# Products of gathered points with their weights: weights copied to PSUM, one instruction for three

## The chip, the cores and the metric

The kernel runs on one core of a Trainium2 chip. Its time is the device time of one launch in microseconds, the median of the runs shown. The profile is of one execution with the hardware profiler on. Engines: TensorE (PE in the profile; PEld its weight loads), VectorE (DVE), ScalarE (ACT), GpSimd (POOL), SyncE (SP).

## The reference

Eight images of 56 x 56 pixels and 128 channels go through four layers. Layers 0, 2 and 3 are deformable convolution blocks; for each pixel, 4 groups x 9 points are read from the projected image at computed places, each as 4 neighbours with bilinear weights, and summed under a softmax mask:

```python
x0 = jnp.floor(ix); y0 = jnp.floor(iy); wx1 = ix - x0; wy1 = iy - y0
samp = corner(y0, x0, (1-wy1)*(1-wx1)) + corner(y0, x0+1, (1-wy1)*wx1) + corner(y0+1, x0, wy1*(1-wx1)) + corner(y0+1, x0+1, wy1*wx1)
y = jnp.einsum('nghwpc,nhwgp->nhwgc', samp, mask).reshape(N, H, W, C) @ w_out + b_out
x = x + gamma1 * layer_norm(y, ...)
x = x + gamma2 * layer_norm(gelu(x @ w_fc1 + b_fc1) @ w_fc2 + b_fc2, ...)
```

Layer 1 is a state space block: four directions, 256 channels, 16 states, with a linear recurrence along all 3136 pixels:

```python
h = h * exp(dt_t[..., None] * A) + (dt_t * u_t)[..., None] * B_t[:, :, None, :]
y = einsum('bkdn,bkn->bkd', h, C_t)
```

All is computed in 32-bit floats.

## The kernel before

**Two streams of work.** There are 24 gather stages (three layers by eight images), and per image one scan of layer 1. The scan of an image is cut into 28 pieces (4 directions x 7 chunks of 448 pixels) by 16 states: 448 scan steps an image, 3584 in all. Gather stages and scan steps of different images run beside each other. The order is written out beforehand: a planner (class `Planner`) emits one list of items, and each engine's program goes through the same list and emits its own part of each item, so the order on each engine is fixed. Semaphores connect the engines.

**A gather stage.** 25 tiles of pixels (24 of 128, one of 64), each in thirds of 12 parts, so 74 units a stage and 1776 in all. POOL (`gpsimd_program`, line 730) issues for each part an indirect DMA that fetches, by an index per partition taken from the SBUF tile d_idx, 128 rows of 512 bytes (4 neighbours x 32 channels) from a table in HBM into the slot d_g; 21168 of them in all. There are five slots. POOL goes through these in order, without regard to the list, and waits for an index group (semaphore idx, made by VectorE at line 1520), and for the slot's last user on TensorE (accq). When a unit has landed, VectorE *weighs* it (item "weigh", line 1325): it multiplies the slot with the weights d_wt, one weight for 32 channels (a step of zero innermost), in place, in three products of 512 elements. TensorE then sums the products by matmuls with the identity into PSUM (item "sum", line 1014, d_p). Item "pr" makes the indices and weights of a group of four tiles in 12 parts; the last of them, part 11, finishes the weights and raises wtr. Items "ch" are the projection, norms and MLP behind it, "ax", "at", "ac" what stands ahead of a stage.

**A scan step** (item "s"; sig counts from -1 to 450 in an image). On VectorE, in order: the scan of half 0 (line 1288; its factor exp(dt*A), `dA0`, lies in PSUM, in columns 0 to 447 of the bank l_pm), the first part of the scan of half 1 (line 1290; its factor, `dA1`, lies in SBUF), the product with B for the next step (line 1301; B lies in the PSUM bank l_pb), the second part of the scan of half 1 (line 1305), and the product with C for the step before (line 1311; C in the PSUM bank l_pc). ScalarE in the same item copies the carry (line 762), computes dA1 for two steps on, and then dA0 for the next step (line 781), which waits until the scan of line 1288 has read the old one. TensorE spreads B and C over the partitions (line 965) and sums the products with C (line 996). Lines 1343 to 1363 (item "h") make dt and dt*u for the next piece.

**What sets the order around the change.** The planner puts a "weigh" after each `pace` scan ticks; so between two scan steps there is at most one, with "ch", "pr", "h" and other items around it; between images and in the first and the last stages weighings follow each other without scan steps. Engine queues are in order. The bank l_pm is written by TensorE in items "p" and "g" too, which come only before and after an image's scan steps. Columns 448 to 511 of the bank aren't used in a scan.

Of the kernel before, what the change touches and what calls it, by code (L numbers as in the profile page):

```python
# [11 lines left out]
ACT = mybir.ActivationFunctionType  # L12
# [22 lines left out]
SLOTS = 5  # L35
# [362 lines left out]
class Mem:  # L398


    def __init__(self, sb, ps, dram, n):
# [80 lines left out]
        self.e = wk[0]  # L482
        self.dt, self.dtu, self.hb = wk[1:3], wk[3:5], wk[8:12]

        self.dA0, self.dA1 = self.pm[:, 0:448], [wk[5][:, 0, :], wk[5][:, 1, :], wk[6][:, 0, :]]
        rows4 = lambda b: b[:, :, :].rearrange("p a b -> p (a b)")[:, 0:512].rearrange("p (t c) -> p t c", c=128)
        self.d, self.sq, self.rv, self.xmt = wk[0], wk[1], wk[2][:, 0, :], wk[2][:, 1, :]
# [24 lines left out]
class Job:  # L512


    def __init__(self, n, order, plan, mem, sems, a, out):
        self.n, self.order, self.plan, self.m, self.s, self.a, self.out = n, order, plan, mem, sems, a, out
        self.use, count = {}, {}
        for item in plan:
            for bank, key in bank_uses(item):
                self.use[key] = count.get(bank, 0)  # L520
                count[bank] = self.use[key] + 1

        self.landed, total = [], [0] * len(GSEMS)
        for Q in range(NQ * len(order)):
            total[Q % len(GSEMS)] += 16 * THIRDS[Q % NQ // 3][Q % NQ % 3]
            self.landed.append(total[Q % len(GSEMS)])
        self.total = total

    def tables(self, T):

# [215 lines left out]
def scalar_program(e, J):  # L746
    m, s = J.m, J.s
# [4 lines left out]
    for item in J.plan:  # L752
        kind = item[0]
        if kind == "s":
# [8 lines left out]
            for q, h in ((0, 1), (1, 1), (0, 0)) if sig == -1 else ((sig + 2, 1), (sig + 1, 0)):  # L763
# [15 lines left out]
                if h == 1 and x >= 3:  # L779
                    e.wait_ge(s["sh"], 2 * x - 4)  # L780
                e.activation(m.dA0 if h == 0 else m.dA1[x % 3], m.dt[P % 2][:, h, :], ACT.Exp,  # L781
                             scale=m.aa[:, kd, h, n:n + 1]).then_inc(s[f"dA{h}"], 1)
        elif kind == "h":
            _, i, j, st = item
            P = 28 * i + j
# [440 lines left out]
def vector_program(e, J):  # L1226
# [30 lines left out]
    for item in J.plan:  # L1257
# [55 lines left out]
        elif kind == "weigh":  # L1313
# [5 lines left out]
            if t % 4 == 0 and u == 0:  # L1319
                e.wait_ge(s["wtr"], G + 1)  # L1320
            e.wait_ge(s[name], count)
            for j in range(0, parts, 4):
                g = m.g[Q % SLOTS][:, j:min(j + 4, parts)].rearrange("p j (r c) -> p (j r) c", c=32)
                wt = bc(m.wt[G % 2][:, t % 4, 12 * u + j:12 * u + min(j + 4, parts)].rearrange("p j r -> p (j r)"), 2, 32)
                ins = e.tensor_tensor(g, g, wt, ALU.mult)  # L1325
            ins.then_inc(s["weighed"], 1)
        elif kind == "h":
# [218 lines left out]
        elif kind == "ch":  # L1546
# [45 lines left out]
PLAIN = ("c_w l_w da xi0 xi1 tab0 tab1 hdo dg htc xr0 xr1 xo0 xo1 vx0 vx1 xn0 xn1 z0 z1 vr0 vr1 vo0 vo1 "  # L1592
         "p_r0 p_r1 p_pm p_pb p_pc f_r0 f_r1 f_pm f_pb f_pc f_a0 f_a1 pa aexp cst dv "
         "weighed accq ysa ytp yta idx wtr w0 pv py exd bst agg sqd x1r xor gbr dgr bsq bnr "
         "dA0 dA1 s1h sh ca accd d1 d2 hd0 md m2 lo ab ex uu qq s1 ln pag psq xir brd lag lsq xmr gsq gt gb tg").split()


def program(nc, a, out, n_img=8, layers=(0, 1, 2, 3)):
# [103 lines left out]
```

## Time and profile before

| | |
|---|---|
| median of 3 runs | 31024.93 us (30998.21 to 31036.17) |
| span of the profiled execution | 31070.8 us |
| PE, PEld busy | 23014.3 us (74%), 14570.5 us (47%) |
| VectorE busy | 23050.6 us (74%) |
| ScalarE busy | 12015.2 us (39%) |
| POOL busy | 23383.1 us (75%) |
| DMA | 1854.55 MB, 60 GB/s |

"Busy" is the time in which an engine executes instructions that are counted. In a list of groups, a row has the line, the engine, the operation, what it writes and reads, the shapes and the count; then the busy time, the mean time of one, and how long the engine was idle just before, with what ended that. "issue" is a pause in which the engine waited for nothing that the profile shows. The timeline merges equal instructions that follow each other (x3). The chain is followed back from the last instruction, at each step to what released it.

### The profile page before, as it was taken

The page shows a single profiled execution, that of the slowest core. Times are in us where ns is not written, and L with a number is a line of the kernel's source. Part 1 is how long each engine was busy: PE and PEld are TensorE (multiplying, and loading weights), DVE is VectorE, ACT ScalarE, POOL GpSimd, SP SyncE. Part 2 cuts the span into 40 slices and gives each one's busy share as a digit, 9 for nine tenths or more (in the row PEclk, how much of TensorE's full clock was granted, in tenths as well). Part 3 has the DMA queues.
Part 4 walks back from the last instruction along what each step waited for, and adds up shares of the span by engine and source line. Part 5 has one row for each costly group of instructions (what it writes and reads, how often), then busy time and mean ns, then how long its engine had stood idle before and what let it go on. Part 6 is the DMA issues. An engine that isn't in the chain of part 4 may idle for free.

```text
span 31070.8 us, 287429 instructions
## 1 busy us (share of the span) xinstructions
PE 23014.3 (74%) x94224; PEld 14570.5 (47%) x94224; DVE 23050.6 (74%) x38816; ACT 12015.2 (39%) x20358; POOL 23383.1 (75%) x21172
## 2 busy tenths in 40 slices
PE   5578778787787778777877787777877787777444
PEld 4444445444544454444544454444544454435433
DVE  1289887888588868888788859886788858885212
ACT  1144444444344434443444434443444444433000
POOL 6777777777677777777777767777677777656767
PEclk7788889888888888888988889888888888888666
DMA  3212122221221221212222121212222121112221
GB/s 75 75 50 64 54 66 65 57 64 51 71 61 51 64 73 51 64 50 57 70 58 63 49 72 53 59 51 64 58 58 61 50 72 52 51 42 67 64 57 53
DMA packets 2410662, 1854.55 MB, mean 60 GB/s; under 512 B 1686546, under 2 KB 2045508, under 8 KB 2409164
## 3 DMA queue, kind: packets, MB, share of 16 engines
q0 software_dynamic: 677376, 1388.62, 16.1%
q1 hardware_dynamic: 1731788, 447.55, 6.5%
q8 instruction: 745, 12.21, 0.2%
q14 instruction: 753, 6.17, 0.1%
HBM read 1569.35 MB, written 265.21 MB: 59 GB/s over the span
## 4 chain that ended last, share of the span: by engine, by line
POOL 61%; issue 18%; PE 12%; DVE 6%; ACT 2%; DMA 1%; SPq 1%; DVEq 0%; POOLq 0%; ACTq 0%
POOL d_g L730 61%; PE d_p L1014 2%; PE d_pr L1162 2%; DVE l_wk L1311 1%; PE l_acc L996 1%; DVE l_wk L1288 1%; DVE d_g L1325 1%; PE d_pr L1049 1%; PE l_pc L1127 1%; DVE l_wk L1305 1%; PE d_pr L1216 1%; DMA d_xin<-mid 0%; SPq L629 0%; DVE l_wk L1290 0%; PE d_pr L1209 0%
## 5 line engine op out<-in xcount | busy, mean ns | idle before, releaser
L730 POOL DMA_INDIRECT d_g<-table,d_idx x21168 | 23382.9, 1105 | 7645.0 <-issue 6426.9
L1014 PE MATMUL d_p<-d_g,c_ident 128*128 128x128 f32 x43200 | 6292.8, 312 | 2702.1 <-DVE d_g L1325 2697.1
L1014 PEld LDWEIGHTS d_p<-d_g,c_ident 128*128 128x128 f32 x43200 | 6108.4, 226 | 3849.1 <-DVE d_g L1325 2820.6
L996 PE MATMUL l_acc<-l_wk,c_ident 128*128 128x448 f32 x14336 | 7295.8, 639 | 436.7 <-DVE l_yx L1276 348.4
L1325 DVE TENSOR_TENSOR d_g<-d_g,d_wt 128x512 f32<-128x512 f32 x5304 | 3361.9, 689 | 3335.2 <-DMA d_g<-table,d_idx 3333.1
L781 ACT ACTIVATE l_pm<-l_wk,l_a 128x448 f32<-128x448 f32 x3584 | 2272.9, 634 | 7292.9 <-DVE l_wk L1288 7287.8
L1301 DVE TENSOR_TENSOR l_wk<-l_wk,l_pb 128x896 f32<-128x896 f32 x3584 | 3824.5, 1067 | 1501.6 <-PE l_pb L965 1499.4
L996 PEld LDWEIGHTS l_acc<-l_wk,c_ident 128*128 128x128 f32 x14336 | 3176.0, 223 | 2507.2 <-issue 2334.0
L1311 DVE TENSOR_TENSOR l_wk<-l_wk,l_pc 128x896 f32<-128x896 f32 x3584 | 3808.2, 1063 | 25.3 <-ACT l_carry L762 21.1
L1288 DVE TENSOR_TENSOR_SCAN l_wk<-l_pm,l_carry,l_wk 128x448 f32<-128x448 f32 x3072 | 3505.4, 1141 | 4.2 <-ACT l_pm L781 1.6
L1305 DVE TENSOR_TENSOR_SCAN l_wk<-l_wk 128x224 f32<-128x224 f32 x3584 | 2432.1, 679 | 0.3
L781 ACT ACTIVATE l_wk<-l_wk,l_a 128x448 f32<-128x448 f32 x3584 | 2362.2, 659 | 17.1 <-DVE l_wk L1357 3.0
L965 PE MATMUL l_pc<-l_spl,c_sel 96*128 96x448 bf16 x3584 | 1424.5, 397 | 1190.4 <-DVE l_wk L1311 1184.1
L1290 DVE TENSOR_TENSOR_SCAN l_wk<-l_wk,l_carry 128x224 f32<-128x224 f32 x3072 | 2026.0, 659 | 0.0
L965 PE MATMUL l_pb<-l_spl,c_sel 96*128 96x448 bf16 x3584 | 1400.9, 391 | 670.5 <-DVE l_wk L1301 668.7
L762 ACT ACTIVATE l_carry<-l_wk 128x2 f32<-128x2 f32 x3584 | 725.9, 203 | 2695.8 <-DVE l_wk L1305 2689.5
L781 ACT ACT_TABLE_LOAD x1181 | 1515.2, 1283 | 21.2
L1162 PE MATMUL d_pr<-d_xt,d_diag 128*128 128x448 f32 x3024 | 1358.5, 593 | 33.9 <-ACT d_xt L889 27.0
L1216 PE MATMUL d_pr<-d_fc,d_ht 128*128 128x128 f32 (+1 forms) x4800 | 903.8, 347 | 546.3 <-ACT d_ht L950 546.2
L965 PEld LDWEIGHTS l_pc<-l_spl,c_sel 96*128 96x128 bf16 x3584 | 369.2, 103 | 1902.7 <-DVE l_wk L1311 1754.3
L1216 PEld LDWEIGHTS d_pr<-d_fc,d_ht 128*128 128x128 f32 (+1 forms) x4800 | 771.6, 242 | 768.5 <-ACT d_ht L950 712.8
L965 PEld LDWEIGHTS l_pb<-l_spl,c_sel 96*128 96x128 bf16 x3584 | 370.2, 103 | 1597.6 <-DVE l_wk L1301 1104.1
(178 smaller groups left out, 22691.0 us busy)
## 6 DMA issues: line engine op xcount, KB each, us to landing
d_g<-table,d_idx POOLq DMA_INDIRECT x21168
table<-d_pst SPq DMA_DIRECT2D x2376, 64.0 KB
hd<-d_hst SPq DMA_DIRECT2D x168, 224.0 KB
d_htc<-hd SPq DMA_DIRECT2D x144, 256.0 KB
d_xin<-mid SPq DMA_DIRECT2D x112, 224.0 KB
mid<-d_xo SPq DMA_DIRECT2D x192, 128.0 KB
d_xres<-mid SPq DMA_DIRECT2D x192, 128.0 KB, 2.2
d_xin<-in_x SPq DMA_DIRECT2D x56, 224.0 KB
```

The source lines that it names most:

```text
L730: e.indirect_dma_start(out=m.g[Q % SLOTS][:, j, :], out_offset=None, in_=m.table[k % 2], in_offset=bass.IndirectOffsetOnAxis(ap=m.idx[G % ...
L781: e.activation(m.dA0 if h == 0 else m.dA1[x % 3], m.dt[P % 2][:, h, :], ACT.Exp, scale=m.aa[:, kd, h, n:n + 1]).then_inc(s[f"dA{h}"], 1)
L965: return e.matmul(bank[:, 0:448], m.sel[:, row + n:row + n + 1].to_broadcast([96, 128]), m.spl[P % 2][:, :], start=True, stop=True)
L996: ins = e.matmul(m.acc[:, h, 0:448], m.ident[:, :], m.hb[x % 4][:, h, :], start=(n == 0), stop=(n == 15))
L1014: ins = e.matmul(m.p0[:, t % 2 * 128:t % 2 * 128 + 32 * w], m.ident[:, :], m.g[Q % SLOTS][:, w * p:w * p + w, 32 * r:32 * r + 32], start=( ...
L1216: e.matmul(bank[0:n, i * 128:i * 128 + 128], m.ht[:, f, i * n:i * n + n], m.fc2[:, f, :], start=(f == 0), stop=False)
L1288: e.tensor_tensor_scan(hb[:, 0, way], m.dA0[:, way], hb[:, 0, way], ini[0], ALU.mult, ALU.add).then_inc(s["sh"], 1)
L1290: e.tensor_tensor_scan(hb[:, 1, one], dA1[:, one], hb[:, 1, one], ini[1], ALU.mult, ALU.add).then_inc(s["s1h"], 1)
L1301: e.tensor_tensor(m.hb[x % 4][:, :, :], m.dtu[P % 2][:, :, :], bc(m.pb[:, 0:448], 1, 2), ALU.mult).then_inc(s["f_pb"], 1)
L1305: e.tensor_tensor_scan(hb[:, 1, two], dA1[:, two], hb[:, 1, two], hb[:, 1, mid:mid + 1], ALU.mult, ALU.add).then_inc(s["sh"], 1)
L1311: e.tensor_tensor(m.hb[x % 4][:, :, :], m.hb[x % 4][:, :, :], bc(m.pc[:, 0:448], 1, 2), ALU.mult).then_inc(s["f_pc"], 1)
L1325: ins = e.tensor_tensor(g, g, wt, ALU.mult)
```

## The change

A weighing that follows a scan step, if that step isn't the last of its image (nor one of those after it), and if its group's weights were finished ahead of the step in the list, takes its weights from PSUM: from columns 448 to 495 of the bank l_pm (`wps`). `find_weights_in_psum` picks these weighings, one at most for a step. ScalarE copies the 48 weights (24 for the unit of six parts) there at the end of its part of that step, behind the exp that makes dA0, and after a wait for wtr. VectorE waits for the new semaphore wps, and multiplies the whole slot in one instruction of 1536 elements instead of three of 512 (768 instead of two for the six parts). Other weighings are as before. The list itself, the gathers and the sums are unchanged.

```diff
+        self.wps = self.pm[:, 448:496]
...
+    def find_weights_in_psum(self):
+
+        self.copied, self.from_psum = {}, {}
+        step, ready = None, set()
+        for item in self.plan:
+            if item[0] == "s":
+                step, ready_then = item[1:], set(ready)
+            elif item[0] == "pr" and item[3] == 11:
+                ready.add(item[1:3])
+            elif item[0] == "weigh" and step and 0 <= step[1] < NSTEP - 1 and step not in self.copied:
+                if (item[1], item[2] // 4) in ready_then:
+                    self.copied[step] = item[1:]
+                    self.from_psum[item[1:]] = len(self.copied)
...
@@ -780,6 +796,13 @@
                 e.activation(m.dA0 if h == 0 else m.dA1[x % 3], m.dt[P % 2][:, h, :], ACT.Exp,
                              scale=m.aa[:, kd, h, n:n + 1]).then_inc(s[f"dA{h}"], 1)
+            if (i, sig) in J.copied:
+                k, t, u = J.copied[i, sig]
+                G = 7 * k + t // 4
+                w = 4 * THIRDS[t][u]
+                e.wait_ge(s["wtr"], G + 1)
+                e.activation(m.wps[:, 0:w], m.wt[G % 2][:, t % 4, 12 * u:12 * u + THIRDS[t][u]].rearrange("p j r -> p (j r)"),
+                             ACT.Copy).then_inc(s["wps"], 1)
...
@@ -1319,9 +1342,15 @@
             e.wait_ge(s[name], count)
-            for j in range(0, parts, 4):
-                g = m.g[Q % SLOTS][:, j:min(j + 4, parts)].rearrange("p j (r c) -> p (j r) c", c=32)
-                wt = bc(m.wt[G % 2][:, t % 4, 12 * u + j:12 * u + min(j + 4, parts)].rearrange("p j r -> p (j r)"), 2, 32)
+            if (k, t, u) in J.from_psum:
+                e.wait_ge(s["wps"], J.from_psum[k, t, u])
+            step = parts if (k, t, u) in J.from_psum else 4
+            for j in range(0, parts, step):
+                g = m.g[Q % SLOTS][:, j:min(j + step, parts)].rearrange("p j (r c) -> p (j r) c", c=32)
+                if (k, t, u) in J.from_psum:
+                    wt = bc(m.wps[:, 0:4 * parts], 2, 32)
+                else:
+                    wt = bc(m.wt[G % 2][:, t % 4, 12 * u + j:12 * u + min(j + 4, parts)].rearrange("p j r -> p (j r)"), 2, 32)
                 ins = e.tensor_tensor(g, g, wt, ALU.mult)
             ins.then_inc(s["weighed"], 1)
```

## Rows read from the trace of the kernel before

**Rows 1.** Busy time by stretch, 1264 to 28700 us.
```profile
core 0: us, PE busy (x) PEld busy (x) DVE busy (x) ACT busy (x) POOL busy (x), PEclk, DMA share, GB/s
1264.00:28700.00 27436.00, 21276.21 (x86259) 13095.51 (x86258) 22310.02 (x36675) 11686.95 (x19793) 20859.79 (x18522) 0.86 0.23 59
```

**Rows 2.** The page's chain that ended last, by engine.
```profile
POOL 61%; issue 18%; PE 12%; DVE 6%; ACT 2%; DMA 1%; SPq 1%; DVEq 0%; POOLq 0%; ACTq 0%
```

**Rows 3.** Waits of POOL: whom it waited for, us in total, times, longest.
```profile
POOL d_g L730 <- issue: 6426.9, 21080, 0.3
POOL d_g L730 <- DVE d_idx L1520: 802.1, 8, 315.5
POOL d_g L730 <- PE d_p L1014: 416.0, 80, 29.7
```

**Rows 4.** Line 730's instructions: duration ns min/median/max, first and last start.
```profile
L730 POOL DMA_INDIRECT d_g<-table,d_idx x21168: 941/947/4515, 153.2 to 31027.4; - x200
```

**Rows 5.** Groups by line, POOL, 170 to 1260 us: busy us, mean ns.
```profile
L730 POOL DMA_INDIRECT d_g<-table,d_idx x866 | 826.8, 955 | 264.0 <-issue 264.0
```

**Rows 6.** Groups by line, POOL, 2500 to 3740 us.
```profile
L730 POOL DMA_INDIRECT d_g<-table,d_idx x873 | 975.5, 1117 | 266.1 <-issue 265.2 <-PE d_p L1014 0.9
```

**Rows 7.** Timeline near 1610 us: start, duration, engine, line, operation.
```profile
1610.04 1.88 DVE L1325 TENSOR_TENSOR d_g<-d_g,d_wt 128x512 f32<-128x512 f32 x3
1610.19 2.55 POOL L730 DMA_INDIRECT d_g<-table,d_idx  x1 [0.30 <-issue]
```

**Rows 8.** Timeline from 10011 us, of DVE, POOL and ACT.
```profile
10011.41 1.15 DVE L1288 TENSOR_TENSOR_SCAN l_wk<-l_pm,l_carry,l_wk 128x448 f32<-128x448 f32 x1
10011.67 0.95 POOL L730 DMA_INDIRECT d_g<-table,d_idx  x1 [0.30 <-issue]
...
10012.59 0.64 ACT L781 ACTIVATE l_pm<-l_wk,l_a 128x448 f32<-128x448 f32 x1 [2.76 <-DVE l_wk L1288]
...
10015.60 1.08 DVE L1349 SCALAR_TENSOR_TENSOR l_wk<-l_wk 128x896 f32<-128x896 f32 x1
...
10015.77 3.55 POOL L730 DMA_INDIRECT d_g<-table,d_idx  x1 [0.30 <-issue]
...
10016.60 1.89 DVE L1325 TENSOR_TENSOR d_g<-d_g,d_wt 128x512 f32<-128x512 f32 x3
```

**Rows 9.** Timeline near 502 us, no scan beside it.
```profile
502.61 0.95 POOL L730 DMA_INDIRECT d_g<-table,d_idx  x1 [0.30 <-issue]
502.64 1.94 DVE L1325 TENSOR_TENSOR d_g<-d_g,d_wt 128x512 f32<-128x512 f32 x3 [11.81 <-DMA d_g<-table,d_idx]
503.86 0.94 POOL L730 DMA_INDIRECT d_g<-table,d_idx  x1 [0.30 <-issue]
```

**Rows 10.** Timeline near 28235 us, POOL.
```profile
28235.87 1.26 POOL L730 DMA_INDIRECT d_g<-table,d_idx  x1 [0.30 <-issue]
```

**Rows 11.** The chain by line, 1264 to 28700 us.
```profile
by line: POOL d_g L730 59.5%; issue 17.6%; PE d_p L1014 2.5%; PE d_pr L1162 1.8%; DVE l_wk L1311 1.1%; PE l_acc L996 1.1%; DVE l_wk L1288 1.1%; DVE d_g L1325 1.0%; PE d_pr L1049 0.9%; PE l_pc L1127 0.8%; DVE l_wk L1305 0.8%; PE d_pr L1216 0
```

**Rows 12.** The chain by line, 10000 to 12000 us.
```profile
by line: POOL d_g L730 19.0%; issue 11.2%; PE d_p L1014 7.9%; PE l_acc L996 5.4%; DVE l_wk L1311 4.5%; DVE l_wk L1288 4.3%; DVE d_g L1325 4.1%; PE d_pr L1162 4.0%; DVE l_wk L1305 3.1%; PE d_pr L1049 2.9%; PE d_pr L1216 2.0%; DVE l_wk L1290 
```

**Rows 13.** Idle time of VectorE before line 1325, 1264 to 28700 us: us, times.
```profile
  DMA d_g<-table,d_idx: 1128.6, 359
```

**Rows 14.** Groups by line, VectorE, whole span: busy us, mean ns, idle before.
```profile
L1301 DVE TENSOR_TENSOR l_wk<-l_wk,l_pb 128x896 f32<-128x896 f32 x3584 | 3824.5, 1067 | 1501.6 <-PE l_pb L965 1499.4
...
L1325 DVE TENSOR_TENSOR d_g<-d_g,d_wt 128x512 f32<-128x512 f32 x5304 | 3361.9, 689 | 3335.2 <-DMA d_g<-table,d_idx 3333.1
...
L1305 DVE TENSOR_TENSOR_SCAN l_wk<-l_wk 128x224 f32<-128x224 f32 x3584 | 2432.1, 679 | 0.3
...
L1353 DVE TENSOR_TENSOR l_wk<-l_wk 128x896 f32<-128x896 f32 x224 | 243.0, 1085 | 0.1
```

**Rows 15.** Groups by line, ScalarE, whole span.
```profile
L781 ACT ACTIVATE l_pm<-l_wk,l_a 128x448 f32<-128x448 f32 x3584 | 2272.9, 634 | 7292.9 <-DVE l_wk L1288 7287.8
...
L762 ACT ACTIVATE l_carry<-l_wk 128x2 f32<-128x2 f32 x3584 | 725.9, 203 | 2695.8 <-DVE l_wk L1305 2689.5 <-issue 1.5
```

More of the change, by code:

```diff
@@ L527, in __init__ @@
         self.total = total
+        self.find_weights_in_psum()
+    def find_weights_in_psum(self):
[10 more added lines that the diff above has]
+                    self.from_psum[item[1:]] = len(self.copied)
     def tables(self, T):
@@ L1594 @@
          "weighed accq ysa ytp yta idx wtr w0 pv py exd bst agg sqd x1r xor gbr dgr bsq bnr "
-         "dA0 dA1 s1h sh ca accd d1 d2 hd0 md m2 lo ab ex uu qq s1 ln pag psq xir brd lag lsq xmr gsq gt gb tg").split()
+         "wps dA0 dA1 s1h sh ca accd d1 d2 hd0 md m2 lo ab ex uu qq s1 ln pag psq xir brd lag lsq xmr gsq gt gb tg").split()
 def program(nc, a, out, n_img=8, layers=(0, 1, 2, 3)):
```

## The prediction

> **What bounds the kernel now.** I read the busy times of the long middle part first, from the start of the second gather stage to the start of the last two: VectorE 22.3, PE 21.3 and GpSimd (POOL) 20.9 of 27.4 ms [rows 1]. None is full, so shares don't decide. The chain that ended last does: POOL 61% and "issue" 18% [rows 2]. POOL only issues the 21168 gathers of one point each (line 730). Its waits [rows 3] say that "issue" is a fixed pause of 0.3 us before nearly every gather (6426.9 us in 21080), and that it waited only 802 us for indices and 416 us for a free slot. So POOL works or pauses for 29.8 of 31.1 ms, and what stretches a gather stretches the kernel, wherever VectorE doesn't lead.
>
> A gather takes 947 ns in the median, 941 at least, but 4515 at most [rows 4], and 1105 in the mean. The stretched part is 21168 x (1105 - 947) = 3.34 ms. Where no scan runs the mean is 955 ns; in a stage with a scan beside it, 1117 [rows 5, 6]. The timeline shows by what. A gather that starts 0.15 us into a weighing lasts 2.55 us, and ends 0.8 us after the weighing [rows 7]. In [rows 8] one that starts 0.26 us into line 1288 takes its 0.95 us, and one that starts in line 1349 and meets the weighing behind it 3.55 us. I went through the whole timeline by what VectorE ran when each gather started: inside a weighing 1670 gathers, 677 us of stretch; inside lines 1305 and 1290 (scans of operands all in SBUF) 5011 and 1122 us; but inside lines 1301 and 1311, which read one operand from PSUM, 2512 and 0 us, and inside line 1288, whose dA is in PSUM, 2233 and 15 us (30 stretched, by what follows). So the stall belongs to VectorE instructions with two SBUF tensors, and lasts until the run of them ends. Phase decides: a gather that starts with the weighing, or between two of its instructions, passes [rows 9].
>
> **The part that moves.** Going through the planner's list by the diff's rule (a weighing behind a scan step that isn't an image's last, its group's weights already made ahead of that step) moves 1347 of the 1776 weighings. The other 429 are in the first and the last two stages, between images, or too early in their group.
>
> *POOL.* In 655 of the 1347 a gather was stretched, the first and last of them in [rows 7] and [rows 10]; the sum is 604 us, 0.45 us per weighing (some cost 1.6, more than half nothing). With one operand in PSUM I expect what lines 1301, 1311 and 1288 show: nothing. Is it moved to the next scans? After weighings with a stall, the next 8.4 us held 0.93 us of stretch, after those without, 0.85. So no: the freed time stays, and 0.08 x 1347 = 108 us may come on top. It counts where the chain runs on POOL: 59.5 + 17.6 = 77% of the stretch that holds the moved weighings [rows 11]; in 10.0 to 12.0 ms it is 30% [rows 12]. 604 x 0.77 = 465 us.
>
> The Trainium skill speaks against this term. Its page "SBUF — State Buffer", section "Who interferes with whom", says that a VectorE instruction with two SBUF inputs contends only with a GpSimd instruction that reads SBUF, and infers from a probe that tensor_tensor doesn't stall descriptor generation. The rows show the opposite for this gather, whose indices lie in SBUF. By the page's inference this term would be 0.
>
> *How much of it can VectorE follow?* In that stretch it waited for gathers 1128.6 us in 359 places [rows 13], 878 us of it at moved weighings, 0.65 us for each. That is more than the 0.45 less its own saving, but unevenly spread: most weighings don't wait at all, and five slots smooth only some 80 us. I keep four fifths: 372 us.
>
> *VectorE.* Three 512-element products take 1.88 to 1.94 us together [rows 7 to 9], 1.89 in the mean of the 1347. One element costs (1085 - 689)/(896 - 512) = 1.03 ns, from lines 1353 and 1325; the fixed part with a PSUM operand is 1067 - 896 x 1.03 = 144 ns, from line 1301 [rows 14]. One 1536-element product: 1582 + 144 = 1.73 us, 0.16 less. 1347 x 0.16 = 211 us. This counts where the chain isn't on POOL: 23%, 49 us. No row shows VectorE reading PSUM with a step of zero innermost (line 1301 repeats 448 columns twice). Bounds: 1.03 ns per element, as line 1325 pays for the same zero step in SBUF, or twice that: (679 - 144)/224 = 2.4 ns is what an element of the slowest kind of instruction there, the scan of line 1305, costs. I take the first, since line 1325 is nearest and line 1301 shows PSUM free; the second is the last rival.
> The same skill, "VectorE: DVE Perf Modes", section on the TRN2 errata, has a higher fixed cost for PSUM sources, which would make the saving an estimated 0.06 us instead; in [rows 14] the PSUM product (1067) is no slower than the SBUF one (1085).
>
> *ScalarE.* 1347 copies of 48 columns into PSUM. Line 762 takes 203 ns for 2 columns, line 781 634 ns for 448 [rows 15]: 0.25 us each, 0.33 ms on an engine that waits 7.3 ms at line 781 alone. The copy stands behind dA0's exp, which can start once scan 1288 is over; its wait for the weights is met by then, since VectorE wrote them ahead of that scan. Queued behind it is ScalarE's own next work, 0.25 us later. In [rows 8] the exp ends at 10013.23, the weighing starts at 10016.60: 3.4 us of cover. Over the 1347 the exp ended 3.4 us ahead in the median, and in only 13 cases less than 0.3 us ahead or later: 13 x 0.6 = 8 us of new wait. The bank isn't written otherwise between a weighing and the next scan. No DMA and no POOL instruction is added; PE waits for the last of a weighing's products as before.
>
> **The sum:** 372 + 49 - 8 = 413 us, 1.33% of the profiled span of 31070.8, so 30658 there. That span is 46 us above the median of the runs, 31024.9, which gives 30610.
>
> **Rivals.**
> *VectorE becomes the bound.* For: it is the busiest engine of [rows 1], in [rows 12] it and PE lead already, and its wait for gathers is 4% of the stretch. Against: that wait exceeds what POOL gains. Then the kernel gains what VectorE gains: 211 us, 30810.
> *POOL keeps everything and the phases get better:* (604 + 108) x 0.77 + 49 = 597 us, 30430. For: after a passed weighing the next gathers were stretched less. Against: uneven waits. The end is where VectorE's waits are used up, 878 + 211, below 29940; I don't reach for it.
> *It does not do what it is for:* POOL's stall doesn't go with the second SBUF operand, the skill's inference above; 49 - 8 = 41 us, 30985, no change. Against: 4745 gathers started in lines 1301, 1311 and 1288 with 15 us of stretch.
> *Slower: the zero step in PSUM costs two cycles.* The product then takes 1536 x 2.06 + 144 = 3.31 us, 1.42 more, 1913 us on VectorE. It decides above 1.89 + 0.65 = 2.54 us, where the waits for gathers are used up: 1913 - 878 = 1035, 32060. For: no row excludes it. Against: PSUM and zero step are each free in [rows 14].
>
> **Chances.** Forecast 0.55, VectorE as bound 0.20, better phases 0.13, no effect on POOL 0.06, slower 0.06. The range takes in the first three: 30350 to 30900. A measurement tells about 0.2%, 62 us, from no change: faster 0.88, same 0.06, slower 0.06.
>
> **What the changed kernel's profile would show.** Right: 1281 of the 5304 products left (1347 weighings had 4023), and 1347 long ones, 1329 of them 128x1536 at 1.7 us; mean gather 1105 down to near 1077 ns, none stretched that starts in a moved weighing; VectorE's wait for gathers down by a few hundred us from 1128.6; POOL's wait for slots up from 416 but by less; ScalarE with 1347 copies of 0.25 us, and hardly a wait of VectorE on them. Wrong: products above 2.5 us; gathers stretched as before inside them; or gathers at 1077 ns and POOL's waits for slots and indices up by as much as it gained.

## The result

The changed kernel takes 30041.17 us (median of four, 30034.11 to 30055.37) against 31023.78 us before: ratio 0.9684, 95% interval 0.967 to 0.9698. The forecast was 30610 with a range down to 30350. The direction is right and the gain is 983 us where 413 had been worked out; the range misses it by 309 us.

The page of the changed kernel, its chain that ended last by engine, beside [rows 2]:

```profile
DVE 35%; PE 29%; POOL 14%; issue 12%; ACT 7%; DMA 1%; SPq 1%; DVEq 0%; ACTq 0%; POOLq 0%
```

POOL and its pause were 79% of the chain and are 26%. VectorE (35%) and PE (29%) lead now. The chain by line in the stretch that holds the moved weighings, 1264 to 27700 us, beside [rows 11]:

```profile
by line: issue 10.9%; DVE l_wk L1334 8.0%; DVE l_wk L1311 8.0%; PE d_p L1037 6.5%; POOL d_g L746 6.1%; PE l_acc L1019 5.8%; DVE l_wk L1328 5.7%; DVE d_g L1354 5.5%; PE d_pr L1185 3.2%; DVE l_wk L1313 2.5%; PE d_pr L1239 2.3%; ACT l_pm L797 
```

(Lines have moved: the gather is L746, was L730; the weighing L1354, was L1325; the scans L1311, L1313 and L1328, were L1288, L1290 and L1305; the products with B and C L1324 and L1334, were L1301 and L1311; dA0's exp L797, was L781; the STT of [rows 8] L1378, was L1349; the sum L1037, was L1014; the indices L1549, was L1520.)

The gathers of the changed kernel, one line's instructions (minimum, median and maximum in ns), beside [rows 4]:

```profile
L746 POOL DMA_INDIRECT d_g<-table,d_idx x21168: 938/944/3818, 155.4 to 29988.7; - x200
```

and POOL's waits in it, beside [rows 3] (us in total, times, longest):

```profile
POOL d_g L746 <- issue: 6395.7, 20986, 0.4
POOL d_g L746 <- DVE d_idx L1549: 1034.2, 17, 341.1
POOL d_g L746 <- PE d_p L1037: 689.1, 165, 29.7
```

The typical gather is as long as before to 3 ns (944, was 947); the mean, in the first row of the next fence, has fallen from 1105 to 1033 ns. POOL's account closes in both kernels: gathers, pauses and waits, and 43 us at the two ends, make the span. Before 23382.9 + 6426.9 + 802.1 + 416.0 + 42.9 = 31070.8; after 21870.2 + 6395.7 + 1034.2 + 689.1 + 42.9 = 30032.1. So the gathers gave 1513 us, and 505 of them came back as waits for indices and slots.

Groups of the changed kernel (busy us, mean ns of one, then idle time ahead and what ended it), beside [rows 14, 15]:

```profile
L746 POOL DMA_INDIRECT d_g<-table,d_idx x21168 | 21870.2, 1033 | 8119.0 <-issue 6395.7
...
L1324 DVE TENSOR_TENSOR l_wk<-l_wk,l_pb 128x896 f32<-128x896 f32 x3584 | 3814.9, 1064 | 1604.7 <-PE l_pb L988 1601.3
L797 ACT ACTIVATE l_pm<-l_wk,l_a 128x448 f32<-128x448 f32 x3584 | 2271.2, 634 | 6232.1 <-DVE l_wk L1311 6219.5
...
L1354 DVE TENSOR_TENSOR d_g<-d_g,d_wt 128x512 f32<-128x512 f32 x1281 | 812.6, 688 | 2291.6 <-DMA d_g<-table,d_idx 2291.3
...
L1354 DVE TENSOR_TENSOR d_g<-d_g,l_pm 128x1536 f32<-128x1536 f32 x1347 | 2330.8, 1730 | 57.2 <-DMA d_g<-table,d_idx 43.5
```

There are 1347 long products of 1730 ns (the 18 short ones of 768 are in the mean). In the stretch from 1264 to 27700 us VectorE's wait for gathers at weighings is nearly gone, 43.5 us at the long ones and 86.7 us at the others, where [rows 13] had 1128.6:

```profile
L1354 DVE TENSOR_TENSOR d_g<-d_g,l_pm 128x1536 f32<-128x1536 f32 x1329 | 2313.9, 1741 | 57.2 <-DMA d_g<-table,d_idx 43.5 <-ACT l_pm L804 7.4 <-issue 4.1
L1354 DVE TENSOR_TENSOR d_g<-d_g,d_wt 128x512 f32<-128x512 f32 x619 | 389.2, 683 | 87.0 <-DMA d_g<-table,d_idx 86.7
```

**Where a gather meets a weighing.** The timeline of the changed kernel at the place of [rows 7] and at a place like that of [rows 8] (start, duration):

```profile
1609.15 1.75 DVE L1354 TENSOR_TENSOR d_g<-d_g,l_pm 128x1536 f32<-128x1536 f32 x1
...
1609.31 0.94 POOL L746 DMA_INDIRECT d_g<-table,d_idx  x1 [0.30 <-issue]
...
1610.56 0.94 POOL L746 DMA_INDIRECT d_g<-table,d_idx  x1 [0.31 <-issue]
...
2018.72 1.08 DVE L1378 SCALAR_TENSOR_TENSOR l_wk<-l_wk 128x896 f32<-128x896 f32 x1
2018.89 1.74 POOL L746 DMA_INDIRECT d_g<-table,d_idx  x1 [0.30 <-issue]
2019.72 1.75 DVE L1354 TENSOR_TENSOR d_g<-d_g,l_pm 128x1536 f32<-128x1536 f32 x1
2020.93 0.94 POOL L746 DMA_INDIRECT d_g<-table,d_idx  x1 [0.30 <-issue]
```

At 1609.31 the gather starts 0.16 us into the long product and takes 0.94 us, where the one of [rows 7], started 0.15 us into three products, took 2.55. The second case is the one that the prediction did not price. The gather at 2018.89 starts in line 1378, two SBUF tensors, and is held by it; but it is let go 0.8 us after that line's end, in the middle of the weighing. In [rows 8] the same pair of instructions held a gather through the weighing too: 3.55 us. I went through both traces by what VectorE ran when each gather started. Stretch is what a gather takes over 947 ns, in us:

| gather started in | before | after |
|---|---|---|
| a weighing | 677 | 73 |
| the 896-wide products of two SBUF tensors (lines 1353, 1349 and their like) | 823 | 530 |
| the scans of half 1 (lines 1290 and 1305) | 1122 | 750 |
| the products of dt with l_xb (lines 1361 and 1363) | 293 | 232 |
| elsewhere | 422 | 239 |
| together | 3337 | 1824 |

In after some 1800 gathers started inside a moved weighing, and none was stretched (the longest took 0.96 us); the 73 us belong to weighings that weren't moved. So the 604 us that the prediction had counted went (677 - 73); and 909 more went in places where nothing was changed.

### The profile page after: what moved, and what is told of

Read it like the earlier page. It is cut to its first block, busy times and chain, and to the rows that moved or that the text cites. A ratio compares the mean times of both kernels' runs of the same rounds, so it can differ in the third digit from the quotient of the medians.

```text
span 30032.1 us, 287320 instructions
## 1 busy us (share of the span) xinstructions
PE 22752.8 (76%) x94224; PEld 14355.0 (48%) x94224; DVE 22824.8 (76%) x36140; ACT 12178.8 (41%) x21705; POOL 21870.4 (73%) x21172
## 4 chain that ended last, share of the span: by engine, by line
DVE 35%; PE 29%; POOL 14%; issue 12%; ACT 7%; DMA 1%; SPq 1%; DVEq 0%; ACTq 0%; POOLq 0%
POOL d_g L746 14%; DVE l_wk L1334 7%; DVE l_wk L1311 7%; PE d_p L1037 6%; PE l_acc L1019 5%; DVE l_wk L1328 5%; DVE d_g L1354 5%; PE d_pr L1185 3%; DVE l_wk L1313 2%; PE d_pr L1239 2%; ACT l_pm L797 2%; PE d_pr L1072 1%; PE d_pr L1051 1%; ACT L973 1%; PE d_pr L1232 1%
## 5 line engine op out<-in xcount | busy, mean ns | idle before, releaser
L746 POOL DMA_INDIRECT d_g<-table,d_idx x21168 | 21870.2, 1033 | 8119.0 <-issue 6395.7
L1037 PE MATMUL d_p<-d_g,c_ident 128*128 128x128 f32 x43200 | 6019.1, 303 | 2046.9 <-DVE d_g L1354 2043.0
L1037 PEld LDWEIGHTS d_p<-d_g,c_ident 128*128 128x128 f32 x43200 | 5874.6, 218 | 3118.9 <-DVE d_g L1354 2149.0
L1324 DVE TENSOR_TENSOR l_wk<-l_wk,l_pb 128x896 f32<-128x896 f32 x3584 | 3814.9, 1064 | 1604.7 <-PE l_pb L988 1601.3
L797 ACT ACTIVATE l_pm<-l_wk,l_a 128x448 f32<-128x448 f32 x3584 | 2271.2, 634 | 6232.1 <-DVE l_wk L1311 6219.5
L1334 DVE TENSOR_TENSOR l_wk<-l_wk,l_pc 128x896 f32<-128x896 f32 x3584 | 3795.0, 1059 | 38.0 <-ACT l_carry L778 24.2
L1311 DVE TENSOR_TENSOR_SCAN l_wk<-l_pm,l_carry,l_wk 128x448 f32<-128x448 f32 x3072 | 3496.9, 1138 | 5.1 <-ACT l_pm L797 2.3
L1354 DVE TENSOR_TENSOR d_g<-d_g,d_wt 128x512 f32<-128x512 f32 x1281 | 812.6, 688 | 2291.6 <-DMA d_g<-table,d_idx 2291.3
L1328 DVE TENSOR_TENSOR_SCAN l_wk<-l_wk 128x224 f32<-128x224 f32 x3584 | 2421.3, 676 | 0.3
L1354 DVE TENSOR_TENSOR d_g<-d_g,l_pm 128x1536 f32<-128x1536 f32 x1347 | 2330.8, 1730 | 57.2 <-DMA d_g<-table,d_idx 43.5
L797 ACT ACTIVATE l_wk<-l_wk,l_a 128x448 f32<-128x448 f32 x3584 | 2359.3, 659 | 17.1 <-DVE l_wk L1386 2.8
L1313 DVE TENSOR_TENSOR_SCAN l_wk<-l_wk,l_carry 128x224 f32<-128x224 f32 x3072 | 2016.8, 657 | 0.0
```

The costliest lines, as they stand in the source:

```text
L746: e.indirect_dma_start(out=m.g[Q % SLOTS][:, j, :], out_offset=None, in_=m.table[k % 2], in_offset=bass.IndirectOffsetOnAxis(ap=m.idx[G % ...
L1037: ins = e.matmul(m.p0[:, t % 2 * 128:t % 2 * 128 + 32 * w], m.ident[:, :], m.g[Q % SLOTS][:, w * p:w * p + w, 32 * r:32 * r + 32], start=( ...
L1311: e.tensor_tensor_scan(hb[:, 0, way], m.dA0[:, way], hb[:, 0, way], ini[0], ALU.mult, ALU.add).then_inc(s["sh"], 1)
L1313: e.tensor_tensor_scan(hb[:, 1, one], dA1[:, one], hb[:, 1, one], ini[1], ALU.mult, ALU.add).then_inc(s["s1h"], 1)
L1324: e.tensor_tensor(m.hb[x % 4][:, :, :], m.dtu[P % 2][:, :, :], bc(m.pb[:, 0:448], 1, 2), ALU.mult).then_inc(s["f_pb"], 1)
L1328: e.tensor_tensor_scan(hb[:, 1, two], dA1[:, two], hb[:, 1, two], hb[:, 1, mid:mid + 1], ALU.mult, ALU.add).then_inc(s["sh"], 1)
```

## The experiments

The kernels ran in four groups, each group on one chip with the kernel before beside it. Each cut of an edit below is against the changed kernel; "..." marks what is left out. The ratios are to the kernel before in the same group; its one profile is that of the rows ahead, and spans and stretches are compared with it. POOL's account for the kernels that tell most (us of the profiled execution; "waits" are those for indices and slots; "stretch" is the gathers' busy time less 21168 x 0.947 us):

| kernel | mean gather, ns | stretch | waits | span | ratio of medians, 95% |
|---|---|---|---|---|---|
| before | 1105 | 3337 | 1218 | 31070.8 | |
| three_psum2 | 1035 | 1873 | 1788 | 30149.7 | 0.9727 (0.971 to 0.9743) |
| one_sbuf2 | 1126 | 3786 | 1212 | 31513.4 | 1.0166 (1.0149 to 1.0183) |
| after3 | 1035 | 1872 | 1671 | 30031.9 | 0.9683 (0.9666 to 0.9699) |
| pad_before | 1094 | 3101 | 1233 | 30847.2 | 0.9941 (0.9925 to 0.9958) |
| behind2 | 1072 | 2638 | 1304 | 30446.1 | 0.9806 (0.9789 to 0.9822) |
| clear2 | 1080 | 2817 | 1300 | 30625.7 | 0.9852 (0.9835 to 0.9868) |
| pad_after2 | 1034 | 1840 | 1851 | 30171.5 | 0.9708 (0.9692 to 0.9724) |
| pace400 | 1029 | 1740 | 2486 | 30732.9 | 0.9887 (0.9871 to 0.9904) |

### The two halves of the change, and the copies alone

`one_sbuf` has one product in place of three, but takes the weights from SBUF and makes no copies:

```diff
-            if (i, sig) in J.copied:
+            if False:
...
-            if (k, t, u) in J.from_psum:
-                e.wait_ge(s["wps"], J.from_psum[k, t, u])
...
-                if (k, t, u) in J.from_psum:
-                    wt = bc(m.wps[:, 0:4 * parts], 2, 32)
-                else:
-                    wt = bc(m.wt[G % 2][:, t % 4, 12 * u + j:12 * u + min(j + 4, parts)].rearrange("p j r -> p (j r)"), 2, 32)
+                wt = bc(m.wt[G % 2][:, t % 4, 12 * u + j:12 * u + min(j + step, parts)].rearrange("p j r -> p (j r)"), 2, 32)
```

> Alone: one product of 1536 elements for three, with the weights still in SBUF; no copies on ScalarE, no new semaphore. Theory (GpSimd's gather is held as long as VectorE runs instructions with two SBUF tensors): VectorE's product gets shorter as in the changed kernel, about 1.74 us for 1.89, but the gap between two products, through which a gather could pass, is gone; stretch of all gathers stays near the 3.34 ms of before or grows, mean gather 1100 to 1130 ns, time 30.95 to 31.3 ms. Rival (the gain comes from the shorter VectorE time and the fewer instructions): 30.0 to 30.3 ms.

`three_psum` has the weights in PSUM, but three products:

```diff
-            step = parts if (k, t, u) in J.from_psum else 4
+            step = 4
...
-                    wt = bc(m.wps[:, 0:4 * parts], 2, 32)
+                    wt = bc(m.wps[:, 4 * j:4 * min(j + 4, parts)], 2, 32)
```

> Alone: weights copied to PSUM, but three products of 512 elements. Theory of the held gather: the mean gather falls as in the changed kernel, to 1030 to 1040 ns, and the time is that of the changed kernel plus what VectorE's 0.15 us more per moved weighing costs where VectorE leads: 30.1 to 30.3 ms. Rival (fewer and longer instructions are the gain): mean gather near 1105 ns, 30.9 to 31.0 ms.

`copy_only` keeps ScalarE's copies and VectorE's wait for them, and weighs in three products from SBUF as before:

```diff
-            step = parts if (k, t, u) in J.from_psum else 4
+            step = 4
...
-                if (k, t, u) in J.from_psum:
-                    wt = bc(m.wps[:, 0:4 * parts], 2, 32)
-                else:
-                    wt = bc(m.wt[G % 2][:, t % 4, 12 * u + j:12 * u + min(j + 4, parts)].rearrange("p j r -> p (j r)"), 2, 32)
+                wt = bc(m.wt[G % 2][:, t % 4, 12 * u + j:12 * u + min(j + 4, parts)].rearrange("p j r -> p (j r)"), 2, 32)
```

> Weighings as before, three products from SBUF, but ScalarE makes the 1347 copies and VectorE waits for them. Theory: copies and waits cost nothing that can be measured, 31.0 to 31.05 ms, 0.25 us a copy. Rival (ScalarE's copies delay something): above 31.1 ms; then the PSUM weights gain more than the changed kernel shows.

Measured: one_sbuf 0.9881 (0.9864 to 0.9897), three_psum 0.9905 (0.9887 to 0.9922), copy_only 1.0006 (0.9991 to 1.002).

In this group of runs and the next the kernel before itself took 35.6 ms and not 31.0, so these ratios are of another balance, and the times in the expectations can't be compared. The page's chain of copy_only, whose gathers are those of the kernel before:

```profile
DVE 35%; another core or an unknown queue 21%; PE 20%; issue 15%; ACT 6%; POOL 1%; SPq 1%; DMA 1%; DVEq 0%; ACTq 0%; POOLq 0%
```

the group of its gathers:

```profile
L746 POOL DMA_INDIRECT d_g<-table,d_idx x21168 | 23389.2, 1105 | 12317.4 <-issue 6216.8
```

and its waits of POOL:

```profile
POOL d_g L746 <- PE d_p L1037: 3552.4, 429, 43.9
POOL d_g L746 <- DVE d_idx L1546: 1508.4, 22, 355.6
POOL d_g L746 <- remote: 1039.4, 324, 11.4
```

The gathers are stretched exactly as before (1105 ns), but POOL waits 3552 us for slots, where [rows 3] has 416, and is 1% of the chain. What a shorter gather frees brings little time there: three_psum, with a mean of 1025 ns, gains 1%. Two things can still be read from this group. The copies and the wait cost nothing that shows (the interval reaches to 0.2%), though VectorE is the leading engine there. And the gathers behave alike in both balances: 1132 ns in one_sbuf, 1025 in three_psum, 1105 in copy_only. That already speaks for the PSUM operand and against the single product as what frees POOL.

### The same, and two subsets, in the second group of runs

`after2` is the changed kernel again. `behind` moves only weighings between which and the scan step VectorE has products of two SBUF tensors from items h, pr or ch (776); `clear` moves only the other 571. The edit of `behind`; `clear` has `not since`:

```diff
                 step, ready_then = item[1:], set(ready)
-            elif item[0] == "pr" and item[3] == 11:
+                since = False
+            elif item[0] == "h" and item[3] in (1, 2, 5, 6, 7, 8) or item[0] == "pr" and item[3] >= 5 or item[0] == "ch" and item[3] in (2, 6, 14, 18):
+                since = True
+            if item[0] == "pr" and item[3] == 11:
                 ready.add(item[1:3])
...
-                if (item[1], item[2] // 4) in ready_then:
+                if (item[1], item[2] // 4) in ready_then and (since):
```

`pad_after` adds to the changed kernel work on VectorE that touches no second SBUF tensor, behind each moved weighing, into columns that nothing reads:

```diff
             ins.then_inc(s["weighed"], 1)
+            if (k, t, u) in J.from_psum:
+                e.memset(m.wk[6][:, 1, 0:192], 0.0)
```

> The changed kernel once more, beside the kernels that split it. All theories: 0.965 to 0.971 of before where the chip shows before at 31.0 ms; where it shows before at 35.7 ms, with long idle stretches of VectorE, the theory that VectorE leads there expects 0.980 to 0.987.

> Moves only the 776 of the 1347 weighings that have an item with a product of two SBUF tensors (parts of h, pr, ch) between them and their scan step. In the trace of before 235 us of stretch belonged to gathers that started inside one of these, and 369 us to gathers that started ahead and were held through it, 604 together. Theory (whole runs of such instructions hold a gather): the sum of stretch falls from 3.34 ms by 600 to 900 us, time 30.4 to 30.65 ms. Rival (only gathers that start inside a weighing count): falls by about 235 us, time 30.8 to 30.9 ms.

> Moves only the other 571 weighings, with no such item ahead. In the trace of before: 369 us of stretch started inside, 71 us held through, 440 together. Theory of the runs: the sum of stretch falls by 440 to 600 us, time 30.6 to 30.8 ms. Rival (only gathers that start inside): falls by about 370 us. If phases are what brings the rest (the scans' own stalls fell by 372 us in the changed kernel), both halves together save clearly less or more than the 1513 us of the whole.

> The changed kernel with one more VectorE instruction behind each moved weighing, a memset of 192 columns of unused space, about 0.25 us, 337 us in all, which reads nothing. Theory (VectorE and PE lead now where the chain of the changed kernel says so, 74% of it): 200 to 340 us longer, 30.25 to 30.4 ms. Rival (POOL leads still): under 100 us longer.

Measured: after2 0.9878 (0.9855 to 0.99), behind 0.9863 (0.9841 to 0.9885), clear 0.9986 (0.9971 to 1.0001), pad_after 0.9884 (0.9862 to 0.9906). The whole change is worth 1.2% in this balance and not 3.2%, as much as one_sbuf in the group before, although their mean gathers are 1020 and 1132 ns. That agrees with the reading above: there POOL isn't the bound, and the PSUM operand has little to give. The stretch of the gathers, 3343 us in copy_only, was 2338 in behind and 2472 in clear, 1005 and 871 us less, where 600 to 900 and 440 to 600 had been expected. pad_after was 13 us longer than after2, and not 200 to 340. Why half of the moved weighings (behind) gave as much as all of them is not settled. None of these four decides anything on the 31.0 ms balance, so they were run again in the groups below.

### The two halves at 31.0 ms

> The changed kernel a third time, beside the parts. On the two chips of the runs so far the kernel before took 35.6 ms, with VectorE and ScalarE idle for up to 80 us at a time without a releaser in the profile, and the changed kernel 0.988 of it; gathers' stretch fell all the same, to 1.54 ms. Where before is at 31.0 ms: 0.966 to 0.971. Where it is at 35.6 ms: 0.984 to 0.992.

> PSUM weights, three products, again. Sum of stretch 1.55 to 1.85 ms whatever the chip. Where before is at 31.0 ms, theory of the held gather: 0.970 to 0.978, most of the whole gain; rival (length and number of products): 0.995 to 1.0.

> One product, SBUF weights, again. Sum of stretch 3.7 to 4.0 ms whatever the chip. Where before is at 31.0 ms, theory of the held gather: 1.0 to 1.015, for POOL leads there and is held longer; rival: 0.97 to 0.98. Where before is at 35.6 ms: 0.985 to 0.992 as before, for VectorE leads there.

Measured, as in the table: the changed kernel 0.9683, PSUM weights alone 0.9727, a single product alone 1.0166. PSUM weights alone bring 856 us of the change's 995. A single product alone, which takes 172 us from VectorE (busy 23050.6 before, 22878.7 in it), makes the kernel 512 us slower. Both results lie at the edge of what was expected: the stretch of three_psum2, 1873 us, is just above its 1.85 ms, and the time of one_sbuf2 just above its 1.015. The page's chain of one_sbuf2, and its gathers:

```profile
POOL 66%; issue 18%; PE 10%; DVE 3%; ACT 2%; DMA 1%; SPq 1%; DVEq 0%; POOLq 0%; ACTq 0%
...
L746 POOL DMA_INDIRECT d_g<-table,d_idx x21168 | 23832.3, 1126 | 7638.2 <-issue 6425.7
```

its long products:

```profile
L1349 DVE TENSOR_TENSOR d_g<-d_g,d_wt 128x1536 f32<-128x1536 f32 x1329 | 2334.1, 1756 | 1451.1 <-DMA d_g<-table,d_idx 1448.1
```

its waits of POOL:

```profile
POOL d_g L746 <- issue: 6425.7, 21085, 0.3
POOL d_g L746 <- DVE d_idx L1544: 795.7, 8, 312.1
POOL d_g L746 <- PE d_p L1037: 416.5, 74, 28.8
```

and its timeline near 1610 us:

```profile
1609.73 1.75 DVE L1349 TENSOR_TENSOR d_g<-d_g,d_wt 128x1536 f32<-128x1536 f32 x1
1609.89 2.41 POOL L746 DMA_INDIRECT d_g<-table,d_idx  x1 [0.30 <-issue]
```

The gather has started 0.16 us into the product, as in after, and lasts 2.41 us, until 0.82 us after its end. Between three products there are two seams at which a gather can slip through; a single product has none. This happens often. Of the gathers of before that started in the first or second product of a moved weighing and were held, 375 were let go 0.82 us after the end of the first or second product, and 356 only after the third. In one_sbuf2 all 1149 that were held by a long product were let go 0.81 to 0.84 us after its end. In the attribution its weighings hold 1010 us of stretch where before had 677, and the scans of half 1 hold 1406 where before had 1122: the closed seams, and then the phases of which the next section speaks. POOL's waits are the same as before to 6 us, so the 449 us of longer gathers make the span 443 us longer. The group of three_psum2's weighings, and its timeline at the same place:

```profile
L1354 DVE TENSOR_TENSOR d_g<-d_g,l_pm 128x512 f32<-128x512 f32 (+1 forms) x4023 | 2502.4, 675 | 58.1 <-DMA d_g<-table,d_idx 44.3 <-ACT l_pm L804 7.9 <-issue 3.9
...
1607.59 1.87 DVE L1354 TENSOR_TENSOR d_g<-d_g,l_pm 128x512 f32<-128x512 f32 x3
1607.76 0.95 POOL L746 DMA_INDIRECT d_g<-table,d_idx  x1 [0.30 <-issue]
```

Three products of the same length as before, only with the weights in PSUM: the gather passes. Of 1923 gathers that started inside a moved weighing of three_psum2 none took more than 0.96 us. It differs from before in the copies and in where the products read 48 numbers, and the copies alone left the stretch as it was (3343 us in copy_only). With both it falls from 3337 to 1873 us. The Trainium skill, "SBUF — State Buffer", section "Who interferes with whom", infers that tensor_tensor doesn't stall the generation of descriptors; for these gathers the runs decide against that inference. They agree with the same section's rule that a VectorE instruction with one SBUF input leaves POOL alone. Which part of a gather's work is held, no run shows.

### VectorE's time alone, with the phases shifted

`pad_before` is three products from SBUF without copies, as before, and the memset of pad_after behind each of the 1347 weighings (the rest of its edit, which leaves out the copies and the PSUM weights, is not shown again):

```diff
             ins.then_inc(s["weighed"], 1)
+            if (k, t, u) in J.from_psum:
+                e.memset(m.wk[6][:, 1, 0:192], 0.0)
```

> The kernel before with a memset of 192 columns, about 0.25 us, on VectorE behind each of the 1347 weighings (three products from SBUF, no copies): 337 us of VectorE. Theory (POOL leads 77% of the stretch in before): under 150 us longer where before is at 31.0 ms, 1.000 to 1.005. Rival (VectorE already leads): 1.008 to 1.011. Where before is at 35.6 ms VectorE leads, 1.000 to 1.010; the changed kernel with the same memset was only 13 us longer there than without, so its price may vanish in idle time.

Measured: 0.9941 (0.9925 to 0.9958). The kernel does 1347 instructions more on an engine that is busy for 74% of the span, and is 183 us faster. I had expected up to 150 us more, and the rival more still; both missed. Its POOL waits:

```profile
POOL d_g L746 <- issue: 6423.3, 21070, 0.3
POOL d_g L746 <- DVE d_idx L1546: 820.7, 9, 316.7
POOL d_g L746 <- PE d_p L1037: 412.6, 88, 28.8
```

These are those of before; the 224 us of span come out of the gathers (stretch 3337 to 3101). No operand and no order was changed. Nor does the memset cut a run short: in before, holds that went on beyond the end of a moved weighing came to 10 us. The stretch in the scans of half 1 fell from 1122 to 936 us, that in the weighings rose from 677 to 747. I read this as the phase. A gather held by the first part of half 1 (line 1290) is let go so that the next one often starts 100 to 200 ns into the second part (line 1305), where it is held again. Such starts, of 3584 scans: 1801 before, 1398 in pad_before, 2214 in one_sbuf2, 1213 in after, 1195 in three_psum2. Where the weighing doesn't hold POOL, and where an instruction of 0.1 us more shifts it, this chain of holds breaks more often. The counts show it; no run sets the phase alone.

### Subsets and padding at 31.0 ms

> The 776 moved weighings behind other products of two SBUF tensors, again. Where before stood at 35.6 ms the sum of stretch fell by 1005 us (of the 604 counted in before). Now with POOL leading in before: stretch down by 850 to 1050 us, and the time by 0.58 of that (as three_psum2 did: 855 us for 1463) plus 776 x 0.16 x 0.66 = 82 us: 0.979 to 0.984. Rival (only gathers that start inside): 235 us, 0.993.

> The other 571, again. Stretch had fallen by 870 us of the 440 counted. Expected now: 650 to 900 us down and 0.982 to 0.988. If stretch falls by 440 or less, the excess belongs to the weighings behind other products; if both halves together fall by more than 1513, they get in each other's way in the whole.

Measured: 0.9806 and 0.9852. The gathers of behind2, then of clear2:

```profile
L749 POOL DMA_INDIRECT d_g<-table,d_idx x21168 | 22684.6, 1072 | 7718.6 <-issue 6414.3
```

```profile
L749 POOL DMA_INDIRECT d_g<-table,d_idx x21168 | 22862.7, 1080 | 7720.1 <-issue 6419.8
```

In the kernel before, the 776 weighings of behind had 235 us of stretch of gathers that started inside them, and 369 us of 202 gathers that had started ahead of them, in the products of h, pr and ch, and were held through; the 571 of clear had 369 and 71 (39 gathers). So a count of both kinds gives 604 and 440, and the stretch fell by 698 and 520: both are 15 to 20% above their count. They are below what I had expected from the 35.6 ms runs (850 to 1050 and 650 to 900), though both times lie in their ranges. A count of starts alone would have made clear the better one by half. It is the smaller. The two together give 1218 us of stretch where the whole gives 1513, and 3.4% of time where it gives 3.2%: stretch adds up to less than the whole, time to a little more.

> The changed kernel plus 337 us of memset on VectorE, now beside pad_before's minus 183 us. If VectorE leads in the changed kernel (chain: POOL and issue only 26 to 29%): 150 to 300 us longer than the changed kernel, 0.973 to 0.978. If POOL still leads: 0.963 to 0.970, for its stretch would fall as in pad_before.

Measured: 0.9708 (0.9692 to 0.9724), 0.25% above after3, some 80 us; by the profiled spans 139 us. The changed kernel wasn't in this group, and the two intervals overlap, so this difference isn't clear of noise. I had expected 150 to 300. The added group:

```profile
L1357 DVE MEMSET l_wk<- 128x192 f32 x1347 | 293.6, 218 | 0.0
```

The mistake lies in that row: 218 ns is its length, but the next scan starts before it is over (at one place of the timeline the memset at 1609.44 us, the scan at 1609.57). VectorE's busy time rises by 132 us only (22824.8 to 22956.7), 0.10 us each. So 132 us of VectorE cost about 80 to 139 us of time. A better price comes from after3 against three_psum2, in one group and with intervals apart: 170 us of VectorE less (22997.5 to 22828.0), 139 us of time. So VectorE's own time now counts at about 0.8, where the prediction had 0.23. In pad_before no cost of the same memset shows; the gathers are the bound there.

`pace400` asks whether a denser series of weighings can take what POOL now waits for. The planner takes the smallest pace at which scan steps are forced in at most 400 ticks, not 40, over the least possible:

```diff
-        if Planner(n, mid).forced <= free + 40:
+        if Planner(n, mid).forced <= free + 400:
```

> The changed kernel with the planner allowed 400 forced ticks over the least, not 40: 1395 moved weighings for 1347, and 152 for 171 left behind the last scan step, where POOL alone leads at about 15 us each: 285 us less there. The 19 weighings and their chains must fit in the scans, where VectorE leads: they cost there what they cost. Expected 0.960 to 0.970; over 0.970 if forced ticks leave gaps.

Measured: 0.9887 (0.9871 to 0.9904), 2% slower than the changed kernel, where 0.960 to 0.970 had been expected. Its waits of POOL:

```profile
POOL d_g L746 <- issue: 6417.9, 21059, 0.4
POOL d_g L746 <- DVE d_idx L1549: 2158.6, 13, 629.4
POOL d_g L746 <- PE d_p L1037: 327.5, 96, 16.8
```

The slots come free sooner (327.5 us, after 689.1), but POOL waits 2158.6 us for indices in 13 places, after 1034.2 in 17, up to 629 us at a time. I take it that what stands between images can't be hidden by weighings that were done sooner; no run tests that. The old pace stays. No kernel tried beats the changed one.

## Why the prediction was wrong in size

**The mechanism holds.** VectorE instructions with two SBUF tensors hold the gathers, one PSUM operand frees them. Of some 1800 gathers that started inside a moved weighing none was stretched; three_psum2 shows it with three products as before: only the operand and the copies are changed, and the copies alone left the stretch as it was. The rival in which POOL isn't helped, at 30985, is out.

**The step that failed is the size of the POOL term.** It counted 604 us, and 1513 went. Of the other 909, 441 were there to be read in the trace of before. The walk through the timeline put each gather to the instruction in which it *started*, and the sum for the moved weighings took only those that started inside one. But the prediction itself says that a stall lasts until the run of instructions ends, and [rows 8] show a gather of 3.55 us that starts ahead of the weighing and is held through it. There are 241 of these at the moved weighings, 441 us in all beyond what the instructions ahead would have held. With them the count is 1045 us; it was possible without a run, and behind2 and clear2 bear it out. The remaining 468 us are a rest that I put to the phases; 64 of them are the 3 ns of the typical gather. The rule was too simple in another place too: about half of the stalls that began in the first two of three products ended at a seam inside the run.

**"Is it moved to the next scans?" was answered from the wrong comparison.** The 0.93 against 0.85 us of stretch after weighings with and without a stall gave 108 us, which the sum then left out. Both kinds of weighing stand in the same kernel, though, one after the other, and the phase with which gathers meet the scans is carried on beyond the 8.4 us that I looked at. The sign was right, the size four times too small, if the whole rest is this. pad_before shows how large such a shift can be with nothing freed at all: 236 us. The share of each place can't be told apart further; that the phases got better and not worse was not to be foreseen from these rows, and the range should have been wider for it.

**The conversion held for this size.** 0.77 x 0.8 = 0.62 of the freed time was to be kept. three_psum2 frees 1463 us and its span is 921 us shorter: 0.63. But that share isn't a constant (the spans hold VectorE's small savings too): clear2 keeps 445 of 520 us, behind2 625 of 698, pad_before 224 of 236, and the longer gathers of one_sbuf2 are paid 443 for 449. For the 604 us that I had, 0.85 to 0.9 would have been right; at 1463 POOL's waits have grown by 569 us, and each further microsecond is worth less. The chain's share of [rows 11] is a price for the first microseconds, and too low even for those. With 1513 us in place of 604 the sum is 1513 x 0.616 + 49 - 8 = 973 us, against a span that is 1039 shorter.

**VectorE.** The long product was to take 1.73 us; it takes 1741 ns with 1536 elements, and 1730 in the mean with the 18 short ones; the zero step innermost in PSUM costs nothing extra, and the slower rival at 32060 is out. The saving was put at 211 us (1347 x 0.16 is 216; the sum moves by 1), and three_psum2 against after3 has 170 us of busy time. It was weighted with 0.23, and brought 139 us, 0.8, since by then VectorE leads. The higher fixed cost of a PSUM source, of the Trainium skill's "VectorE: DVE Perf Modes", TRN2 errata, would have made that product slower than one from SBUF. It is not seen: the same product takes 1741 ns from PSUM and 1756 from SBUF, in one_sbuf2. The waits of VectorE for gathers fell not "by a few hundred" but from 1128.6 to 130 us. That is nearly the end that the second rival named, below 29940, where these waits are used up.

**ScalarE.** The copies, the changed kernel's group by line:

```profile
L804 ACT ACTIVATE l_pm<-d_wt 128x48 f32<-128x48 f32 x1347 | 260.6, 193 | 0.0
```

0.19 us each, not 0.25, and VectorE waited 7.4 us for them, where 8 were expected. copy_only shows no cost of them, at 35.6 ms.

**The rivals.** *VectorE becomes the bound* came true as a statement on the chain, 35% and with PE 64%, but after POOL's gain and not in its place. *POOL keeps everything and the phases get better* was the right one in kind; its 30430 rested on 604 + 108 us, and was too small by the same missing terms.

## To carry to other kernels

A stall that lasts until a run of instructions ends must be counted by its end and not by its start: list the gathers that overlap the instruction that you change, also those that began before it. Where a free-running engine beats against a fixed pattern, a small change of the pattern can move the sum by hundreds of microseconds either way (here 236 less in pad_before, and 284 more in the scans of one_sbuf2), so widen the range for it, and price a saving in the pattern together with the seams that it closes (one product in place of three was 1.7% slower on its own). The share of an engine in the chain that ended last is a poor price for a change of it: by it 0.62 of the freed time was to be kept, where changes of 236 to 698 us kept 0.86 to 0.95 and the one of 1463 us 0.63. An account of its busy time, pauses and waits shows what a large one leaves.

## What the runs showed of the hardware

- An indirect gather that starts from about 0.1 us after the start of a run of VectorE instructions with two SBUF tensors up to about 0.2 us before its end lasts until 0.76 us after the end of a scan, or 0.82 us after that of a product. Instructions back to back can hold it as one run, but of 731 gathers held from the first two of three products 375 were let go at a seam. Closing the seams (one_sbuf2) brought 449 us of stretch, of which 333 lie in the weighings.
- VectorE starts an instruction before the one ahead is over: a memset of 218 ns adds 0.10 us of busy time, and three products of 689 ns take 1.89 us together. Durations of short instructions are not what they cost.
- The same kernel before took 35.6 ms in two groups of runs and 31.0 in two and in the first result; one chip showed both. In the traces of the long ones VectorE was idle for more than 20 us at a time 111 to 135 times, 4.5 to 5.3 ms in all, against 17 times and 0.62 ms in before; the chain has 19 to 21% "another core or an unknown queue", and POOL waits for "remote" (1039.4 us above), which the short ones don't have. What held it is open; no run was made for it.
